# A ternary feed forward inside a four-layer transformer kernel: the channel maximum in one operation, normalising and rounding on ScalarE, and new orders on all engines

## The reference

```python
def act_quant(x):
    scale = 127.0 / jnp.clip(jnp.max(jnp.abs(x), axis=-1, keepdims=True), 1e-05)
    return jnp.clip(jnp.round(x * scale), -128, 127) / scale
def weight_quant(w):
    scale = 1.0 / jnp.clip(jnp.mean(jnp.abs(w)), 1e-05)
    return jnp.clip(jnp.round(w * scale), -1, 1) / scale
# bit_linear(x, w): act_quant(x) times weight_quant(w)
h = bit_linear(x, w1)                      # 256 -> 1024 channels
h = depthwise_conv1d(h, conv_w, conv_b)    # three taps along the rows
h = jax.nn.silu(h)
return bit_linear(h, w2)                   # 1024 -> 256, added to the residual
```

## Time and profile before

| what | value |
|---|---|
| median of 3 runs | 5345.92 us (5342.0 to 5346.08) |
| the profiled execution's own time | 5337.01 us |
| its span, first to last instruction | 5335.2 us |
| mean granted TensorE clock | 0.944 of full |
| busy share of the span: PE, DVE, ACT, POOL | 86%, 63%, 37%, 34% |
| the touched stage in the span | about 620 to 1335 us |

### The profile page before, as it was taken

The page is one execution under the profiler, slowest core; times in us unless marked ns, Lnnn a source line. Parts: engine busy times, 40 slices in busy tenths (PEclk is TensorE's granted clock), DMA queues, the critical chain, the costliest instruction groups (busy, mean ns, idle before and its releaser), DMA issues. The chain is left out here.

```text
span 5335.2 us, 92076 instructions
## 1 busy us (share of the span) xinstructions
PE 4608.6 (86%) x32476; PEld 3589.8 (67%) x32476; DVE 3361.5 (63%) x9943; ACT 1966.4 (37%) x4118; POOL 1811.2 (34%) x2246
## 2 busy tenths in 40 slices
PE   7888565656989699979998799999999977999978
PEld 5666344434868588866776688888888844778845
DVE  6999677777845333217886477777777753444344
ACT  3444233344434332215554233333333323222234
POOL 2222123333325423225552133333333222555522
PEclk9999878888989899989999899999999988999989
DMA  4666401111632322222221211101011036222233
GB/s 113 146 149 139 113 29 39 40 36 44 181 91 60 51 74 86 66 58 66 73 76 36 74 31 31 35 29 29 29 31 31 25 107 222 82 85 94 74 94 107
DMA packets 329714, 397.17 MB, mean 74 GB/s; under 512 B 66021, under 2 KB 289994, under 8 KB 318506
## 3 DMA queue, kind: packets, MB, share of 16 engines
q1 hardware_dynamic: 315946, 366.04, 24.2%
q0 software_dynamic: 13312, 25.25, 2.0%
HBM read 297.64 MB, written 93.55 MB: 73 GB/s over the span
## 5 line engine op out<-in xcount | busy, mean ns | idle before, releaser
L2528 PE MATMUL fa_h<-fa_xnT,fa_w 128*128 128x256 f32 x2048 | 484.9, 382 | 0.0
L2540 PE MATMUL fa_y<-fa_w,fa_hT 128*128 128x256 f32 x2048 | 462.5, 379 | 0.0
L2540 PEld LDWEIGHTS fa_y<-fa_w,fa_hT 128*128 128x128 f32 x2048 | 386.8, 190 | 65.0 <-issue 14.8
L2528 PEld LDWEIGHTS fa_h<-fa_xnT,fa_w 128*128 128x128 f32 x2048 | 382.2, 190 | 71.1 <-issue 13.2
L1013 PE MATMUL f_c_ps<-f_hs,f_diag 64*64 64x256 f32 x3072 | 229.7, 456 | 219.8 <-DVE f_hs L863 219.8
L2407 ACT ACTIVATE fa_hT<-fa_h,fa_b 128x256 f32<-128x256 f32 x512 | 214.6, 470 | 543.9 <-PE fa_h L2528 481.9
L1013 PEld LDWEIGHTS f_c_ps<-f_hs,f_diag 64*64 64x64 f32 x3072 | 133.1, 164 | 299.9 <-DVE f_hs L863 226.8
L423 DVE TENSOR_REDUCE a_mx<-a_score 128x16 f32<-128x1920 f32 x128 | 275.8, 2155 | 55.0 <-PE a_score L607 55.0
L2914 ACT ACTIVATE m_hT<-m_h,m_b 128x256 f32<-128x256 f32 x256 | 107.3, 470 | 404.0 <-PE m_h L2951 404.0
L1554 PE MATMUL r_h<-r_xnT,r_rw 128*128 128x256 f32 x1024 | 247.1, 390 | 0.7 <-ACT r_xnT L1504 0.7
L940 ACT ACTIVATE f_y<-f_c_ps,f_cbias 128x256 f32<-128x256 f32 x256 | 100.2, 474 | 373.5 <-PE f_c_ps L1013 373.4
(11 more groups left out here) (451 smaller groups left out, 11262.9 us busy)
## 6 DMA issues: line engine op xcount, KB each, us to landing
a_floor<-a_lowest SPq DMA_DIRECT2D x64, 960.0 KB, 8.3
cv_toep<-kernels SPq DMA_DIRECT2D x16, 2048.0 KB, 9.5
x<-a_xo SPq DMA_DIRECT2D x96, 256.0 KB, 4.1
f_xb<-x SPq DMA_DIRECT2D x64, 256.0 KB, 3.0
f_xres<-x SPq DMA_DIRECT2D x64, 256.0 KB, 3.0
a_xb<-x SPq DMA_DIRECT2D x64, 256.0 KB, 3.1
e_w<-in_L_ffn_ew SPq DMA_DIRECT2D x16, 1024.0 KB, 7.4
a_cb<-in_ctx SPq DMA_DIRECT2D x96, 90.0 KB, 1.9
```

What stands on the lines that cost most here:

```text
L2528: last = pe.matmul(h_ps[j % 2][:, c, :], w1[:, e, k, f:f + P], xnT[it.p][:, k, :], start=k == 0, stop=k == KD - 1)
L2540: last = pe.matmul(bank[:, t * D:(t + 1) * D], hT[e % 2][:, k, t * P:(t + 1) * P], w2[:, e, k, :], start=k == 0, stop=k == KE - 1)
```

## The change

Magnitude and channel maximum become one tensor_reduce of DVE over y, read with the channel block innermost; ACT's magnitudes and DVE's five tensor_tensor operations per item go. Normalising moves from DVE to ACT (Identity with scale and bias from a new DVE operation `less_mean`). The multiplication by 127 goes: the clipped maximum is multiplied by 1/127 in the same operation. DVE's rounding of y moves to ACT; the clip at 127 is done by ACT's Relu on MAGIC + 127 minus y, so the operand of `down` is 127 - q, the second weights are negated, and a product of a constant -127 with the column sums of the weights (computed once) repairs the sum. `quantise` is cut in five steps, and the lists of POOL, DVE, ACT and PE get new orders. SP's list stays.

```diff
-                    sp.wait_ge(quant, QN * (it.i - 2) + 2)
+                    sp.wait_ge(xn_ready, TL * (it.i - 1))
...
-                (5, spread(dg2, hscale, hq, HQ, dg2_ready, row2_done)), (5, scale_hidden), (1, roots_of),
-                (2, spread(dg, ainv, quant, QN, dg_ready, row_done))], unroll=4, history=4)
+                (1, roots_of), (5, spread(dg2, hscale, hq, HQ, HQ, dg2_ready, row2_done)),
+                (2, spread(dg, ainv, quant, QN, AINV, dg_ready, row_done)), (5, scale_hidden)], unroll=4, history=4)
...
+                dve.tensor_scalar(wq[:].rearrange("p k n -> p (k n)"), wf[:], -1.0, 1.0 - 2.0 * m, ALU.max, ALU.mult).then_inc(w_all, 1)
+            dve.wait_ge(w_all, 8)
+            dve.tensor_reduce(wf[:, 0:D], w2q[:].rearrange("p k d -> p d k"), AX.X, ALU.add).then_inc(w_all, 1)
+            dve.wait_ge(w_all, 9)
+            dve.tensor_copy(w2sum[:], wf[:, 0:D]).then_inc(w_all, 1)
...
+            def less_mean(it):
+                dve.wait_ge(roots, 2 * it.i + 2)
+                dve.scalar_tensor_tensor(minus[p][:], mv[p][:, :, 0], -1.0, rs[p][:, :, 0], ALU.mult, ALU.mult).then_inc(minus_ready, 1)
+            def row_max(it):
+                dve.wait_ge(xn_ready, TL * (it.i + 1))
...
+                c.add(dve.tensor_reduce(amax[p][:], xn[p][:], AX.X, ALU.max, apply_absolute_value=True))
+            def row_step(it):
+                c.wait()
+                c.add(dve.tensor_scalar(amax[p][:], amax[p][:], 1e-5, 1.0 / STEPS, ALU.max, ALU.mult))
+            def row_scale(it):
+                c.wait()
+                c.add(dve.reciprocal(ascale[p][:], amax[p][:]))
+                c.wait()
+                for t in range(TL):
+                    c.add(dve.tensor_scalar(xn[p][:, t, :], xn[p][:, t, :], ascale[p][:, t:t + 1], MAGIC, ALU.mult, ALU.add))
+                c.add(dve.tensor_scalar(ainv[p][:], amax[p][:], wmean[:, 0:1], None, ALU.mult))
             def quantise(it):
...
+                c.add(dve.tensor_scalar(qx[p][:], xn[p][:], MAGIC, STEPS, ALU.subtract, ALU.min))
...
+            def hidden_max(it):
+                dve.wait_ge(silu_ready, KH * (it.i + 1))
+                dve.tensor_reduce(pmax[it.p][:], y[it.at][:].rearrange("p k s -> p s k"), AX.X, ALU.max, apply_absolute_value=True).then_inc(pmax_ready, 1)
...
-            def round_hidden(it):
-                dve.wait_ge(multiplied, it.i + 1)
-                dve.tensor_scalar(y[it.at][:], y[it.at][:], MAGIC, MAGIC + 127.0, ALU.add, ALU.min).then_inc(scaled, 1)
...
-                (4, h_out(0)), (4, h_out(1)), (5, hidden_max(1)), (6, round_hidden), (1, norm_stats), (5, hidden_scale), (4, h_out(2)),
-                (2, quantise), (4, h_out(3)), (7, y_out), (4, hidden_max(0))], unroll=4, history=4)
+                (2, less_mean), (1, norm_stats), (4, h_out(0)), (4, h_out(1)), (5, hidden_max), (2, row_max), (2, row_step), (5, hidden_scale),
+                (4, h_out(2)), (4, h_out(3)), (2, row_scale), (7, y_out), (2, quantise)], unroll=4, history=4)
...
+            def norm(it):
+                act.wait_ge(minus_ready, it.i + 1)
...
+                for t in range(TL):
+                    act.activation(xn[p][:, t, :], xb[p][:, t, :], ACT.Identity, bias=minus[p][:, t:t + 1], scale=rs[p][:, t, :]).then_inc(xn_ready, 1)
...
+            def round_hidden(it):
+                act.wait_ge(multiplied, it.i + 1)
+                act.activation(y[it.at][:], y[it.at][:], ACT.Copy, bias=MAGIC).then_inc(rounded, 1)
+            def below_top(it):
+                act.wait_ge(rounded, it.i + 1)
...
+                act.activation(qh[it.p][:], y[it.at][:], ACT.Relu, bias=top[:, 0:1], scale=-1.0).then_inc(qh_ready, 1)
...
-                (4, silu(0)), (3, row_out(aux, row, row_done, row_ready, h_ready, 4)), (4, sizes(0)),
-                (5, row_out(aux2, row2, row2_done, row2_ready, multiplied, 1)), (3, turn_out), (6, quantised), (4, silu(1)), (4, sizes(1))], unroll=4, history=4)
+                (2, norm), (6, round_hidden), (4, silu(0)), (3, turn_out), (6, below_top), (5, row_out(aux2, row2, row2_done, row2_ready, multiplied, 1)),
+                (3, row_out(aux, row, row_done, row_ready, h_ready, 4)), (4, silu(1))], unroll=4, history=4)
...
-            pe.wait_ge(w_all, 8)
+            pe.wait_ge(w_all, 10)
...
-                        last = pe.matmul(y_ps[:, t, :], qh[it.p][:, k, t * P:(t + 1) * P], w2q[:, k, :], start=k == 0, stop=k == KH - 1)
+                        pe.matmul(y_ps[:, t, :], qh[it.p][:, k, t * P:(t + 1) * P], w2q[:, k, :], start=k == 0, stop=False)
+                    last = pe.matmul(y_ps[:, t, :], low[:], w2sum[:], start=False, stop=True)
...
-                (4, up(0)), (3, turn), (4, up(1)), (7, down), (4, conv(0)), (5, turn_max), (4, up(2)), (4, up(3)),
+                (4, up(0)), (4, up(1)), (7, down), (4, conv(0)), (5, turn_max), (4, up(2)), (4, up(3)), (3, turn),
                 (3, make_row(aux, dg, dg_ready, row_done, row_ready)), (5, make_row(aux2, dg2, dg2_ready, row2_done, row2_ready)), (4, conv(1))], unroll=4, history=4)
```

More of the change, by code:

```diff
@@ L68, with __init__ @@
 class Chain:
-    def __init__(self, eng, sem, i, per):
-        self.eng, self.sem, self.base, self.per, self.n = eng, sem, i * per, per, 0
+    def __init__(self, eng, sem, i, per, n=0):
+        self.eng, self.sem, self.base, self.per, self.n = eng, sem, i * per, per, n
     def add(self, ins):
@@ L719, in ternary_feed_forward @@
     pmax = [st.sb(f"pmax{p}", [P, S]) for p in two]
-    yabs = st.sb("yabs", [P, KH, S])
-    pair, best = ([st.sb(f"{n}{m}", [P, k, S]) for m in two] for n, k in (("pair", 2), ("best", 1)))
+    minus = [st.sb(f"minus{p}", [P, TL]) for p in two]
+    w2sum, low, top = st.sb("w2sum", [P, D], BF16), st.sb("low", [P, P], BF16), st.sb("top", [P, 1])
     qh = [st.sb(f"qh{p}", [P, KH, S], BF16) for p in two]
@@ L731, in ternary_feed_forward @@
         st.sem(n) for n in ("h_done", "h_ready", "c_done", "silu_ready", "pmax_ready", "pmax_turned", "hq", "dg2_ready", "row2_done", "row2_ready"))
-    multiplied, abs_ready, maxed = st.sem("multiplied"), st.sem("abs_ready"), st.sem("maxed")
+    multiplied, minus_ready, xn_ready, rounded = (st.sem(n) for n in ("multiplied", "minus_ready", "xn_ready", "rounded"))
     folded = st.sem("folded")
-    UNITS, MADE = 2, 4 + KH * 3
+    UNITS, MADE = 2, 6 + KH * 3
     scaled, qh_ready, y_done, y_ready = (st.sem(n) for n in ("scaled", "qh_ready", "y_done", "y_ready"))
-    QN = 10
-    HQ = 4
+    QN, AINV = 7, 6
+    HQ = 3
+    STEPS = 127.0
     DEPTH = 8
@@ L770, in _ @@
         def _(pool):
+            pool.memset(low[:], -STEPS).then_inc(consts, 1)
+            pool.memset(top[:], MAGIC + STEPS).then_inc(consts, 1)
             for p in two:
@@ L784, in roots_of, with spread @@
                 inverse_root(pool, Chain(pool, roots, it.i, 2), mv[it.p][:, :, 1], rs[it.p][:, :, 0], const)
-            def spread(out, scale, ready, links, done, used):
+            def spread(out, scale, ready, links, link, done, used):
                 def step(it):
-                    pool.wait_ge(ready, links * (it.i + 1))
+                    pool.wait_ge(ready, links * it.i + link)
                     if it.reused():
@@ L830, in norm_stats @@
                 layer_norm_stats(dve, Chain(dve, stats, it.i, 4), xb[it.p], stt[it.p], mv[it.p], const)
-            def quantise(it):
+            def less_mean(it):
                 p = it.p
                 dve.wait_ge(roots, 2 * it.i + 2)
+                dve.scalar_tensor_tensor(minus[p][:], mv[p][:, :, 0], -1.0, rs[p][:, :, 0], ALU.mult, ALU.mult).then_inc(minus_ready, 1)
+            def row_max(it):
+                p = it.p
+                dve.wait_ge(xn_ready, TL * (it.i + 1))
+                if it.reused():
+                    dve.wait_ge(dg_ready, it.i - 1)
+                    dve.wait_ge(turned, it.i - 1)
                 c = Chain(dve, quant, it.i, QN)
-                for ins in normalise(dve, xb[p], mv[p], rs[p][:, :, 0], xn[p]):
-                    c.add(ins)
+                c.add(dve.tensor_reduce(amax[p][:], xn[p][:], AX.X, ALU.max, apply_absolute_value=True))
+            def row_step(it):
+                p = it.p
+                c = Chain(dve, quant, it.i, QN, 1)
                 c.wait()
-                c.add(dve.tensor_reduce(amax[p][:], xn[p][:], AX.X, ALU.max, apply_absolute_value=True))
-                c.wait()
-                c.add(dve.tensor_scalar(amax[p][:], amax[p][:], 1e-5, None, ALU.max))
+                c.add(dve.tensor_scalar(amax[p][:], amax[p][:], 1e-5, 1.0 / STEPS, ALU.max, ALU.mult))
+            def row_scale(it):
+                p = it.p
+                c = Chain(dve, quant, it.i, QN, 2)
                 c.wait()
@@ L844, in quantise @@
                 c.wait()
[L845 to L849, removed]
                 for t in range(TL):
                     c.add(dve.tensor_scalar(xn[p][:, t, :], xn[p][:, t, :], ascale[p][:, t:t + 1], MAGIC, ALU.mult, ALU.add))
```

(29 more changed lines are left out.)

10 lines of the change are left out of this document (removed).

## The result

| | before | after |
|---|---|---|
| median | 5343.96 us | 5186.74 us |
| ratio, 95% interval | | 0.9707 (0.9695 to 0.972) |
| profiled execution, its span | 5337.01, 5335.2 us | 5188.26, 5186.4 us |

A forecast was written before the change was run, and what follows sets the result against it. A loop through several engines, with DVE's clip held by POOL, was taken as the bound. POOL's 31 intervals fall from 622.9 to 402 us; with +1 and +1.2 in all -219, so 5345.9 becomes 5127 us, range 5090 to 5180.

The forecast's parts named there:

- What bounds: Software-pipelined stage: a loop through several engines; DVE's clip, held by POOL 4.48 us, delays h_out(3), conv(1) waits 7.31 us.
- Items 1 to 3: Slot from T, the end of turn_max: h_out(3) ends T+2.2, y_out starts T+3.16, PE's conv(1) to down done T+8.5.
- Item 8: The lock: quantise and less_mean pass beside POOL's 4.5 us multiplication, which starts at T+4.1; later DVE work is not held.
- The rival: The lock moves: POOL wins against quantise or less_mean, next T at 14.6 to 14.9, 5161 us; chance 0.25.
- Item 6: hidden_max, a reduce with 1 KB step: 2.29 us, hidden behind conv(0) with 0.5 us to spare; bounds 2.2 and 4.6.
- Items 4 and 5: DVE's statistics wait for x, landing T+7.76; h_out(1) ends T+10.15, then conv(0) and turn_max, next T at T+13.4.
- The clock: Rival: strided reduce or low clock ahead of conv(0), next T at about 15.2, 45 us more, 5172; chance 0.12.
- item 5: After x lands: h_out(1) ends T+10.15, conv(0) takes 2.82 us at full clock, turn_max 0.44, next T at T+13.4.
- The sum: POOL's 31 intervals 402 us, before 622.9; once +1 for the column sum ahead, +1.2 for the tail; in all -219.

The follow-up runs named there:

- the single moved step: Kernel before with only h_out(3) put ahead of quantise in DVE's list: ratio 0.9778 to before; 31 intervals of POOL's multiplication (S) 507.3 us, where 622.9 were.
- flat: Changed kernel with the hidden maximum reading its elements contiguously, over neighbouring rows: ratio 0.9658 to the kernel before, S 445.0 us.
- moved: Changed kernel with less_mean moved on DVE to behind h_out(3) of the slot before: ratio 0.9643 to the kernel before, S 438.0 us.

## Why the prediction was wrong

- **What bounds** was right: the held clip ahead of h_out(3) was the bound, shown by the single moved step (116 us of S).
- **Items 1 to 3** held: from the end of turn_max at 926.30, y_out starts at 929.24, T+2.94 (forecast 3.16), quantise at T+3.73 (3.95), POOL's multiplication at T+3.99 (4.1).
- **Item 8 failed.** "I take both as passing" was right for quantise, wrong for less_mean. The order of the starts was forecast to 0.2 us, but what was concluded from the earlier trace rows, that two such DVE operations back to back keep POOL out, does not carry over: POOL asked at 930.29 while quantise ran, and won against less_mean at 930.36. Rows 4 had the case that fits. What the hold does to the slot: h_out(1) ends at T+10.8 where T+10.15 was forecast, which alone makes 14.1 us of 13.4, as ten slots of "flat" show. The rival had 0.25 and 5161. Its 14.6 us was worked out for a held quantise, with 0.4 us of less_mean behind it; for the held less_mean it is 0.5 too much, and 5161 is still too fast, because of the next two points.
- **Item 6 failed**, mis-sized: 2.29 taken, 3.7 measured. The row was read against the wrong standard. The copy of line 2649 took 1.16 us for 1024 elements, but line 898, a one-source operation of DVE between SBUF tiles like that copy, took 1.22 for 2048: the step had probably made the copy slow, and comparing its rate with that of the reduce hid it. (That the step made the copy slow is argued from these two rows; no run has that copy without the step. That it made the reduce slow is shown.) The rule of the Trainium skill's page "SBUF — State Buffer", section "Door 1: The DMA port swizzle", stood against the change and was the better guide: 3.7 us with the step, 2.28 without. With the hold, the reduce puts the next T at T+14.95 (10.8, 3.7 and 0.44).
- **Items 4 and 5** were right in mechanism: with hold and stride taken away DVE waits 3.3 us for x and the slot is 13.15 (13.4). In the changed kernel the hold covers it (four waits, 1.7 us in all).
- **The clock** was a rival at 0.12, together with the reduce. PE waits 2.9 us ahead of conv(0), which then takes 4.1 to 4.5 us in 16 of 25 slots, item 5's 2.82 in nine. Hold, reduce and clock were priced as alternatives; they came together, and the range, built from one at a time, did not hold their sum. The 25 slots take 15.6 us on average, 2.2 above item 5's 13.4: about 0.7 is the hold, 0.85 the reduce and 0.6 the slow conv(0), each counted on top of the one before it, as an estimate from the slots above.
- **The sum** outside the loop: from the first weight reduce to the first multiplication 57.7 us before, 59.5 after (+1.8, forecast +1; the column sum is itself a strided reduce, 3.6 us); behind the last multiplication +1.1 (forecast +1.2). The stage itself began 6 us later in the profiled execution after. Its first weight reduce starts anywhere from 638.1 to 649.9 us in the traces of the changed kernel and its variants, which all have the same stages ahead of it, so the 6 us lie within that spread.

Open: what exactly decides between POOL and a DVE operation that follows another without a wait (the two pairs of the earlier trace rows differ), and why slots of one kernel have now a fast and now a slow conv(0) behind the same wait. A hidden maximum that is exact and reads without steps was not tried.

## What to carry to other kernels

When a held operation is freed by a new order, list every DVE operation that will lie beside POOL's long ones, by form: tensor_scalar between SBUF tiles and operations with two SBUF tensors were held, even at 2 elements a partition (4.48 and 4.50 us); reductions, statistics, the products with a PSUM input and tensor_scalar of a single element were not. Then ask what the hold had covered: here the x of the next item, worth 84 us of S once the hold was gone and at most 5 to 7 before, where the intervals of the times tell no difference. Price a strided read against the same operation unstrided, and where several rivals can be true together, work out the slot with all of them: here they gave 51 us together, 21 and 14 alone.

## What the runs showed of the hardware that was not expected

- A two-element product of two SBUF tensors waited 4.50 us for POOL, and the same product as two single elements took 0.33 us in the midst of the same POOL operation; beside another, a tensor_scalar of 4 elements with a per-partition operand was held (0.49 us) and one of a single element was not (0.14 us).
- The step of a reduce costs nothing at 8 bytes and nearly the same from 16 bytes to 1 KB (2.28 against 3.7 to 3.9 us).
- The length of PE's wait did not settle how long conv(0) took: in the changed kernel waits of 2.85 to 2.87 us were followed by 2.82 us in some slots and by 4.1 to 4.5 in others, a wait of 3.72 by 2.83; in "moved" a wait of 1.97 us was followed by 4.51.
